# Two-layer attention, scan and expert block on one core: projections in 128 and 64 rows, maxima regrouped, identity products, scan inputs on DVE

## The reference

```
x += cross_attention(LN(x), ctx)      # L0: 16 heads of 16, K and V = ctx @ Wk, ctx @ Wv
x += state_space(LN(x))               # conv of 4 taps, softplus, scan over 128 tokens, 16 states
x += attention_and_experts(LN(x))     # one small attention, 8 gated experts of 1024
x += cross_attention(LN(x), ctx)      # L1: other weights, the same context
x += linear_attention(LN(x))          # three projections, softmax weights, conv, MLP
x += set_experts(LN(x))               # 64 slots picked by a maximum, two small products
```

## Time and profile before

| | us |
|---|---|
| median of 3 runs | 1336.77 |
| lowest, highest | 1335.69, 1338.14 |
| the profiled execution | 1334.81 |
| its span, first to last instruction | 1332.7 |
| TensorE busy | 1192.7 |
| DVE busy | 714.2 |
| ACT busy | 715.0 |
| POOL busy | 224.8 |

### The profile page before, as it was taken

How to read it: one execution, slowest core, us unless ns; L and a number is a source line. 1 busy time by engine, 2 the same in 40 slices (tenths; PEclk the granted TensorE clock), 3 DMA queues, 4 the chain that set the end, 5 groups by cost and what they waited for, 6 DMA issues and landing times.

```text
span 1332.7 us, 29487 instructions
## 1 busy us (share of the span) xinstructions
PE 1192.7 (89%) x12749; PEld 768.2 (58%) x12749; DVE 714.2 (54%) x1351; ACT 715.0 (54%) x995; POOL 224.8 (17%) x118
## 2 busy tenths in 40 slices
PE   8999999999999999316699899999999999999566
PEld 6356666666666666206598356666555666666344
DVE  2565555555555663668223546555555555575332
ACT  3356666666666667242213356666666666667322
POOL 0222122222222200033000222222222211110000
PEclk9699999999999999557799799999999999999668
DMA  8444444444433360610803744444433334360540
GB/s 187 115 105 105 105 105 105 105 101 88 101 89 88 68 171 2 217 63 0 314 2 90 174 104 105 105 102 88 98 83 90 86 86 104 84 160 3 205 135 5
DMA packets 80947, 138.18 MB, mean 104 GB/s; under 512 B 9064, under 2 KB 72176, under 8 KB 80304
## 3 DMA queue, kind: packets, MB, share of 16 engines
q1 hardware_dynamic: 79920, 136.16, 41.2%
q10 hardware_dynamic: 896, 0.12, 0.1%
HBM read 57.96 MB, written 0.15 MB: 44 GB/s over the span
## 4 chain that ended last, share of the span: by engine, by line
PE 76%; DVE 17%; ACT 2%; DMA 2%; issue 2%; POOL 0%; SPq 0%; ACTq 0%; DVEq 0%; POOLq 0%
PE ring L543 41%; PE st L543 17%; PE ot L543 15%; DVE mpart L1221 9%; DVE arena L1348 2%; DMA qst<-rowb 2%; PE ring L674 1%; DVE arena L1352 1%; ACT arena L932 1%; PE ring L549 0%; PE ring L642 0%; DVE work L1342 0%; DMA warena<-ctxT 0%; POOL arena L532 0%; DVE work L1296 0%
## 5 line engine op out<-in xcount | busy, mean ns | idle before, releaser
L1221 DVE TENSOR_REDUCE mpart<-ring 128x1 f32<-128x448 f32 x896 | 515.8, 618 | 402.2 <-PE ring L543 400.0
L955 ACT ACTIVATE work<-st 128x1024 f32<-128x1024 f32 x392 | 401.2, 1023 | 169.5 <-PE st L543 165.2
L543 PE MATMUL ring<-arena,qst 96*128 96x448 bf16 x896 | 298.6, 367 | 4.3 <-DVE mpart L1221 2.5
L543 PE MATMUL ot<-work,arena 128*17 128x128 f32 x6272 | 247.5, 275 | 2.1 <-ACT work L955 1.1
L543 PE MATMUL st<-qst,arena 97*128 97x128 bf16 x3136 | 241.1, 219 | 5.8 <-DMA qst<-rowb 5.4
L543 PEld LDWEIGHTS st<-qst,arena 97*128 97x128 bf16 x3136 | 196.1, 98 | 67.7 <-issue 29.2
L543 PEld LDWEIGHTS ot<-work,arena 128*17 128x17 f32 x6272 | 137.6, 96 | 142.1 <-issue 94.3
L495 POOL TENSOR_TENSOR arena<-arena 128x896 f32<-128x896 f32 x52 | 98.2, 1888 | 692.1 <-ACT arena L928 692.0
L543 PE MATMUL ring<-warena,wkv 96*128 96x448 f32 x448 | 192.1, 558 | 1.5 <-DVE mpart L1221 1.3
L543 PE MATMUL ring<-wkv,warena 96*128 96x256 f32 x784 | 188.4, 383 | 1.0 <-DVE mpart L1221 1.0
L543 PEld LDWEIGHTS ring<-wkv,warena 96*128 96x128 f32 x784 | 146.2, 190 | 28.2 <-DVE mpart L1221 11.3
(11 more groups left out here) (278 smaller groups left out, 640.3 us busy)
## 6 DMA issues: line engine op xcount, KB each, us to landing
arena<-arena SPq DMA_DIRECT2D x336, 224.0 KB, 5.1
warena<-ctxT SPq DMA_DIRECT2D x28, 672.0 KB, 5.0
arena<-ffn_W SPq DMA_DIRECT2D x16, 1024.0 KB, 12.4
arena<-f SPq DMA_DIRECT2D x2, 4096.0 KB, 24.3
arena<-scratch_bc SPq DMA_DIRECT2D x1, 2048.0 KB, 6.9
arena<-rows SPq DMA_DIRECT2D x1, 1792.0 KB, 6.8
warena<-w_in_proj SPq DMA_DIRECT2D x1, 1024.0 KB
warena<-w_W SPq DMA_DIRECT2D x1, 1024.0 KB, 6.9
```

The source lines that it names most:

```text
L543: return nc.tensor.matmul(o, l, r, start=start, stop=stop, **kw)
L955: nc.scalar.activation(pbuf[:, n % 2], st[:, 2 * (n % 2):2 * (n % 2) + 2].rearrange("p b k -> p (b k)"), ACT.Exp).then_inc(*signal(f"{lay} ...
L1221: V.reduce_max(mpart[:, 2 * h + hf:2 * h + hf + 1], ring[:, BANKS[step][0], 0:HALF], AX_X).then_inc(*signal(f"{lay}_b_max"))
```

## The change

1. **Row halves.** The 192 channels are contracted as 128 + 64. The 64-row tail of the context and of wkv is loaded twice, to partitions 0 to 63 and 64 to 127. Steps come in pairs: the full-height matmuls of both, then the tails, one on the lower and one on the upper half of the rows, into the two banks of the pair. The semaphore of both steps is raised by 2 at the end of the pair.
2. **Order.** v pairs stand in units 0 and 2, k pairs in 5 and 7. Maxima are 1,3,1,3,3,1,3,1,3 and 3,2,3,2,3 (19 in nine units, 13 in five). In the start of the plan the keys of a chunk stand in pairs too.
3. **Identity products** in `mamba`, `ffn`, `linear_attention` and `sets`, ahead of waits.
4. **Scan inputs** are made by DVE. The gate's reciprocal is cut in two and moved behind x_proj and behind sp_u, its product behind the first scan input.

```diff
+TAIL = CC - P
+STACKED = SLOTS * HD
+PROJECTION_LOADS = 3
-    plan = [("k", 0, 0), ("k", 0, 1), ("k1", 0, 0), ("k", 0, 2), ("k2", 0, 0), ("k", 0, 3), ("k1", 0, 1), ("k2", 0, 1)]
+    plan = [("k", 0, 0), ("k", 0, 1), ("k1", 0, 0), ("k", 0, 2), ("k", 0, 3), ("k2", 0, 0), ("k1", 0, 1), ("k2", 0, 1)]
...
-    plan += some(2 * H, 0) + [("row", 0, 0)] + [("k", 2, n) for n in range(3)] + score(0) + [("k", 2, 3)] + score(1)
-    values = {u: u for u in range(4)}
-    keys = {5: 0, 6: 1, 7: 2, 8: 3}
+    plan += some(2 * H, 0) + [("row", 0, 0)] + [("k", 2, n) for n in range(2)] + score(0) + [("k", 2, n) for n in range(2, 4)] + score(1)
+    values = {0: (0, 1), 2: (2, 3)}
+    keys = {5: (0, 1), 7: (2, 3)}
-        per_unit = ((4,) * 8 + (0,) if c == 0 else (1, 1, 1, 1, 3, 2, 2, 2, 2)) + (3, 4, 3, 4, 3)
+        per_unit = ((4,) * 8 + (0,) if c == 0 else (1, 3, 1, 3, 3, 1, 3, 1, 3)) + (3, 2, 3, 2, 3)
...
-        wkv = sb("wkv", [CP, 2, 2, D])
-        qst = sb("qst", [CP + 1, 2, H, TOK], BF16)
+        wkv = sb("wkv", [P, 2, 2, D])
+        qst = sb("qst", [STACKED + 1, 2, H, TOK], BF16)
...
+        TAILS = (slice(0, TAIL), slice(TAIL, P))
...
-                for n in range(2):
-                    load(wkv[:, :, n], a[f"{lay}_wkv"][n].rearrange("(k p) n -> p k n", p=CP), f"{lay}_wkv_in")
+                load(wkv[:, 0], a[f"{lay}_wkv"][:, 0:P].rearrange("n p d -> p n d"), f"{lay}_wkv_in")
+                for part in range(2):
+                    load(wkv[part * TAIL:(part + 1) * TAIL, 1], a[f"{lay}_wkv"][:, P:CC].rearrange("n p d -> p n d"),
+                         f"{lay}_wkv_in")
...
-                load(ctxt[0:CP, par], a["ctxT"].rearrange("(k p) n -> p k n", p=CP)[:, :, bass.ds(at, CK)],
-                     f"{lay}_ctx_in{par}")
+                load(ctxt[:, par, 0], a["ctxT"][0:P, at:at + CK], f"{lay}_ctx_in{par}")
+                for part in range(2):
+                    load(ctxt[part * TAIL:(part + 1) * TAIL, par, 1], a["ctxT"][P:CC, at:at + CK],
+                         f"{lay}_ctx_in{par}")
...
-            pool.wait_ge(*done_of("dtu_ready"))
-            pool.wait_ge(sem("bc_in"), 16)
-            for b in range(NB):
-                if b >= 2:
-                    pool.wait_ge(sem("scanned"), b - 1)
-                nc.gpsimd.tensor_tensor(
-                    m_["dBu"][:, b % 2].rearrange("p (n t) -> p n t", n=NS),
...
-            def keep_clock(n):
+            def keep_clock(n, bank=4):
                 for _ in range(n):
-                    mm(pb[4][:, 0:P], ident, ident)
+                    mm(pb[bank][:, 0:P], ident, ident)
...
-                        project(ring[:, bank, 0:HALF], lambda k: wkv[:, k, 0, m * P:(m + 1) * P],
-                                lambda k: ctxt[0:CP, c % 2, k, hf * HALF:(hf + 1) * HALF], f"{lay}_k_full", 2)
+                        mm(ring[:, bank, 0:HALF], wkv[:, 0, 0, m * P:(m + 1) * P],
+                           ctxt[:, c % 2, 0, hf * HALF:(hf + 1) * HALF], stop=False, skip_group_check=True)
+                        if hf:
+                            for half, rows_of in enumerate(TAILS):
+                                last = mm(ring[:, BANKS[(kind, c, n - 1 + half)][0], 0:HALF],
+                                          wkv[rows_of, 1, 0, m * P:(m + 1) * P],
+                                          ctxt[rows_of, c % 2, 1, half * HALF:(half + 1) * HALF], start=False,
+                                          skip_group_check=True)
+                            last.then_inc(sem(f"{lay}_k_full"), 2)
                     if kind == "v":
                         for t in range(2 * n, min(2 * n + 2, TPC)):
-                            last = project(ring[:, bank, (t % 2) * D:(t % 2 + 1) * D],
-                                           lambda k: ctxt[0:CP, c % 2, k, t * P:(t + 1) * P],
-                                           lambda k: wkv[:, k, 1, :], None, 2)
-                        last.then_inc(*signal(f"{lay}_v_full"))
+                            mm(ring[:, bank, (t % 2) * D:(t % 2 + 1) * D], ctxt[:, c % 2, 0, t * P:(t + 1) * P],
+                               wkv[:, 0, 1], start=(t % 2 == 0), stop=False, skip_group_check=True)
+                        if n % 2:
+                            for t in (2 * n - 2, 2 * n, 2 * n - 1, 2 * n + 1):
+                                if t < TPC:
+                                    rows_of = TAILS[t // 2 % 2]
+                                    last = mm(ring[:, BANKS[(kind, c, t // 2)][0], (t % 2) * D:(t % 2 + 1) * D],
+                                              ctxt[rows_of, c % 2, 1, t * P:(t + 1) * P], wkv[rows_of, 1, 1],
+                                              start=False, skip_group_check=True)
+                            last.then_inc(sem(f"{lay}_v_full"), 2)
...
             def mamba():
+                keep_clock(11, 6)
                 transpose2(tmp[0], 5, "rms_normed", "rmsT_full")
...
+                keep_clock(30, 6)
                 pe.wait_ge(*done_of("xi_ready"))
...
+                    if b == NB - 1:
+                        keep_clock(14, 6)
                     pe.wait_ge(sem("weighted"), b + 1)
...
+                keep_clock(3, 6)
                 pe.wait_ge(*done_of("y_ready"))
...
-                dve.wait_ge(*done_of("res_exp"))
-                sigmoid_of_exp(m2["sres"])
-                link(V.tensor_tensor(m2["sres"].rearrange("p b t -> p (b t)"), pb[1][:, :],
-                                     m2["sres"].rearrange("p b t -> p (b t)"), ALU.mult))
...
                 V.tensor_copy(m_["bcT"][RANK:RANK + 2 * NS], pb[2][RANK:RANK + 2 * NS, 0:TOK]).then_inc(*signal("bcT_ready"))
+                dve.wait_ge(*done_of("res_exp"))
+                link(V.tensor_scalar(m2["sres"], m2["sres"], 1.0, None, ALU.add))
+                V.reciprocal(m2["sres"][:, 0:NB // 2], m2["sres"][:, 0:NB // 2])
...
                 dve.wait_ge(*done_of("sp_u"))
+                link(V.reciprocal(m2["sres"][:, NB // 2:], m2["sres"][:, NB // 2:]))
...
+                def inputs(b):
+                    V.tensor_tensor(m_["dBu"][:, b % 2].rearrange("p (n t) -> p n t", n=NS),
+                                    m3["dtu"][:, b:b + 1].broadcast_to([P, NS, TOK]),
+                                    m_["bc"][:, 0:NS * TOK].rearrange("p (n t) -> p n t", n=NS), ALU.mult
+                                    ).then_inc(sem("dBu_ready"), 1)
...
+                dve.wait_ge(sem("bc_in"), 16)
+                inputs(0)
+                link(V.tensor_tensor(m2["sres"].rearrange("p b t -> p (b t)"), pb[1][:, :],
+                                     m2["sres"].rearrange("p b t -> p (b t)"), ALU.mult))
...
+                    if b + 1 < NB:
+                        inputs(b + 1)
                     dve.wait_ge(sem("weighted"), b + 1)
```

More of the change, by code:

```diff
@@ L33 @@
 CC = 192
-CP = 96
+TAIL = CC - P
 H = 16
@@ L127, in score @@
         return [("s", g // UNITS, g % UNITS), ("e", g // UNITS, g % UNITS)] if g < NCH * UNITS else []
-    plan = [("k", 0, 0), ("k", 0, 1), ("k1", 0, 0), ("k", 0, 2), ("k2", 0, 0), ("k", 0, 3), ("k1", 0, 1), ("k2", 0, 1)]
+    plan = [("k", 0, 0), ("k", 0, 1), ("k1", 0, 0), ("k", 0, 2), ("k", 0, 3), ("k2", 0, 0), ("k1", 0, 1), ("k2", 0, 1)]
     plan += [("v", 0, n) for n in range(4)] + [("k", 1, n) for n in range(4)] + [("v", 1, n) for n in range(4)]
     plan += [("k1", 1, 0), ("k1", 1, 1), ("k2", 1, 0), ("k2", 1, 1)]
-    plan += some(2 * H, 0) + [("row", 0, 0)] + [("k", 2, n) for n in range(3)] + score(0) + [("k", 2, 3)] + score(1)
-    values = {u: u for u in range(4)}
-    keys = {5: 0, 6: 1, 7: 2, 8: 3}
+    plan += some(2 * H, 0) + [("row", 0, 0)] + [("k", 2, n) for n in range(2)] + score(0) + [("k", 2, n) for n in range(2, 4)] + score(1)
+    values = {0: (0, 1), 2: (2, 3)}
+    keys = {5: (0, 1), 7: (2, 3)}
     firsts, seconds = {7: 0, 9: 1}, {10: 0, 11: 1}
     for c in range(NCH):
-        per_unit = ((4,) * 8 + (0,) if c == 0 else (1, 1, 1, 1, 3, 2, 2, 2, 2)) + (3, 4, 3, 4, 3)
+        per_unit = ((4,) * 8 + (0,) if c == 0 else (1, 3, 1, 3, 3, 1, 3, 1, 3)) + (3, 2, 3, 2, 3)
         for u in range(UNITS):
             if c + 2 < NCH and u in values:
-                plan.append(("v", c + 2, values[u]))
+                plan += [("v", c + 2, n) for n in values[u]]
             if c + 3 < NCH and u in keys:
-                plan.append(("k", c + 3, keys[u]))
+                plan += [("k", c + 3, n) for n in keys[u]]
             plan.append(("pv", c, u))
@@ L415, in attention_loads @@
                 sp.wait_ge(sem(f"{lay}_ones_set"), 1)
-                load(arena[CP:CP + 1, A_KST:A_V].rearrange("p (n k) -> p n k", k=HALF), ones, f"{lay}_ones_in")
+                load(arena[STACKED:STACKED + 1, A_KST:A_V].rearrange("p (n k) -> p n k", k=HALF), ones, f"{lay}_ones_in")
                 sp.wait_ge(*done_of(f"{lay}_q_split"))
@@ L577, in general_path @@
                     with pe.Fori(0, TILES) as t:
-                        pe.wait_ge(sem("g_ctx_in"), 16 * t + 16)
```

(15 more changed lines are left out.)

29 lines of the change are left out of this document (20 added, 9 removed).

## The result

The changed kernel takes 1354.3 us (median of 4 runs, 1353.99 to 1356.03), the kernel before 1337.45 beside it: a ratio of 1.0121 [1.0101, 1.0141], the brackets giving the 95% interval. It is 1.2% slower; 1266 had been predicted, and the range ended at 1300. The profiled execution took 1356.03, with a span of 1353.9.

A forecast was written before the change was run, and what follows sets the result against it. TensorE's instructions were taken to bound the attention loops, all three engines' chain the rest. Savings of 43.5 (loops), 11 (state-space) and 15.6 (identity products) sum to 70: from 1334.81 to 1264.7, median 1266; range 1240 to 1300.

The forecast's parts named there:

- the back stretch in part 2: Chunk's stretch up to the next chunk's scores: they wait 1.2 for the row of maxima; stretch becomes 12.55, +1.0.
- Landing 1.9 later: DMA of the row of maxima, sent by ACT: lands 1.9 us after its issue, as in the earlier trace.
- the 2.35: End of the back stretch: TensorE's work following the scores' wait for the row takes 2.35 us.
- Row halves, full overlap: Key and value matmuls in a chunk: two 64-row tails run at once, saving 2.79 us a chunk.
- Rival (a): Tails in the 112 pairs: halves do not overlap, 78 us is lost, time 1344; chance 6%.
- Entering and leaving the form: Switching to row halves: entering costs .2, leaving nothing new where pv follows; four pairs a chunk, +.8 us.
- Front stretch: Chunk's part with value sets and key pairs: 2.7 us less, becoming 21.5.
- Prologue and chunk 0 together: Ahead of each attention loop and in its first chunk: -6.8 us for both prologues, -1.0 for each first chunk.
- Rival (b): Value tails: weight loads bound them, costing 37 us, time 1303, or 1285 halfway; chance 14%.
- Rival (c): Wait for the row in steady chunks: ACT is not late, 20 x 1.2 comes back, time 1242; chance 12%.
- Rival (d): Stages outside the loops: identity products do not lift the clock, 15.6 us gain becomes +3, time 1285; chance 8%.
- part 3: State-space stage: moved sigmoid, scan inputs on DVE instead of POOL, and fuller clock make it 11 us shorter.

The follow-up runs named there:

- the maxima earlier: Changed kernel with the maxima per unit reordered so a chunk's last maximum precedes POOL's first subtraction: 1327.81 us, ratio .9925.
- all three: Changed kernel with ACT's row step ahead of the second key copies, SP's stack load held until the row landed, and maxima earlier: 1257.47 us, ratio .9409.
- the row step first: Changed kernel with ACT's row step of unit 10 ahead of its second key cast instead of behind it: 1273.65 us, ratio .9518.

## Why the prediction was wrong

**The step that failed** is the back stretch in part 2: "row copy 7.98, issue 8.26, landed and seen 10.2. The scores wait 1.2, and with the 2.35 that follow the stretch becomes 12.55". It had the right chain and the right waiting instruction, and three of its terms were off (from the prediction's zero, 357.87 in the chunk shown):

- The row copy came at 8.71, not 7.98: +.73. Up to the cast at 363.30 ACT was on the layout (5.43 for 5.4). The exponential that had been placed at 6.25 came at 6.96, because its scores were late: TensorE had stood .71 for maxima, with DVE held by POOL. With that hold gone (the maxima earlier) the row copy comes 1.06 sooner. I put starts side by side for ACT and none for POOL; of DVE the prediction says only that it "has less to do in the back stretch", although `nmb` of before ran just .19 behind POOL's subtraction.
- "Landing 1.9 later" was taken over from the earlier trace rows. It holds for a row ahead of the stack load (the median of before is 1.7). Behind it, it is 3.2: +1.25. My layout moved the issue by some 1.4 against the keys, and I didn't ask what else was issued there: SP's queue was in the text with its context loads alone.
- The work after the wait, 2.35, took 3.88, because the wait brought the clock down: +1.5. With the wait filled and the clock up the same work takes 2.39, so the 2.35 was right for full clock. I priced the wait as idle time only, although had shown me what a light stretch does to the clock, and the identity products were priced on just that.

Together 10.2 + .73 + 1.25 is the 12.19 at which the scores start, and with 3.88 the 16.07 of the trace. Over twenty steady chunks 38.39 - 34.0 is 88; the sum missed by 91 (1264.7 against 1356.03).

**Point by point.**
- Row halves, full overlap: right, 80 to 82.5 measured without, 78 by the sum. Rival (a), the only one on the slow side, was wrong; the time was as if it were right.
- Entering and leaving the form: right. A key pair to the next pv is 2.65 in after; the sum had 2.25 + .2, and the .09 ahead of any pv. The missing .11 stands in the pair's first pass.
- Front stretch: 21.83 in the chunk shown, and at full clock a median of 21.9, for 21.5.
- Prologue and chunk 0 together, with the late row repaired (all three): -5.9 in L0 and -3.9 in L1 for -4.1 and -3.0. In after itself, where chunk 0 has the late row too, -1.0 and +1.7.
- Rival (b), weight loads: no sign of it. A value set of 16 passes takes 2.96, where twelve passes of .215, the tail of .16 and one entry of .2 make 2.94.
- Rival (c), ACT is not late: the opposite. The range treated that wait as something that could only get shorter.
- Rival (d) was wrong, the products hold the clock. 22.6 measured; with the clock terms of part 3 the sum had 17.3. The 5 between them is about what the ffn and the stages behind L1, without products, take more than in before.
- Part 3: -12.5 for -11; without the products -7.9 for -9.3.
- Two slips in the sums change little: four passes of 512 columns are 1.7, not 1.3, and 1264.7 + 1.96 is 1266.7.

With the row step first the change gives 1273.65, 8 above the forecast. That nearness is in part luck: the forecast holds 1.2 of wait for the row in each steady chunk, and this kernel has .07, with .72 of wait for the held maxima in its place. The kernel with neither, 1257.47, is to be laid beside the sum without its wait, 1242: the work was priced 15 too low, some .6 a steady chunk, of which .4 is the front stretch. That alone would have left the forecast in its range. What put it outside was the one place where DVE's hold, ACT's order and SP's loads meet.

## What to carry to other kernels

A small DMA that TensorE waits for should be issued ahead of everything that may stand before it: ahead of casts on its own engine, and ahead of large loads on other queues. When a change shifts the engines against each other, list for each late step what other engines run or issue within half a microsecond of it in the old trace (here .19 and .33): those margins are the change's real risk. And a wait on TensorE is to be priced with the clock behind it: here 1.95 of idle cost 1.7 more.

## What was not expected of the hardware

- A small DMA (4 KB, from ACT) lands 1.7 us behind its issue when a burst of 224 KB loads is issued .3 us behind it, 2.9 to 3.2 when the burst is .5 to .2 ahead.
- A two-input DVE operation on 16 columns, .17 alone, takes .82 under a POOL subtraction of 1.89, until that ends.
- Around idle waits of about 1.95 in an otherwise busy loop, the clock fell to 1.2 GHz 22 times out of 22; around waits of about 1.6 (a few of them longer), 16 times out of 22; around waits of .2, never. Eight identity products in the wait prevented it. A single wait of 1.88 in another kernel left it up.
- Two 64-row f32 matmuls of 448 columns on different row halves take the time of one: .75 less per pair of keys, in which two such overlaps of .375 lie. Their starts are .007 apart.
